# Row buffers and one-hot matrices of the edge stage of a graph layer: six buffers of one tile, one-hot matrices made by twos

## What is computed

```python
msgs = x[src]
out = x @ root + bias
for r in range(R):
    mask = (edge_type == r)
    sums = segment_sum(msgs * mask[:, None], dst, N)
    cnt = segment_sum(mask, dst, N)
    out = out + (sums / maximum(cnt, 1)[:, None]) @ weight[r]
z = concat([out, x], 1) @ w_gate + b_gate
h = tanh(out) * z + x * (1 - z)
```

## Time and profile before

| what | value |
|---|---|
| median of three runs | 1840.62 us (1838.92 to 1841.84) |
| the profiled execution, its own time | 1834.11 us |
| its span, first to last instruction | 1832.4 us |
| PE busy | 1708.7 us (93%) in 7873 matmuls |
| DVE busy | 1096.1 us (60%) in 1444 instructions |
| ACT busy | 727.0 us (40%) |
| POOL busy | 749.1 us (41%) |
| mean granted PE clock | 0.972 |
| moved by DMA | 339.69 MB, mean 185 GB/s |

### The profile page before, as it was taken

How to read it: one execution, slowest core, us unless ns; L and a number is a source line. 1 busy time by engine, 2 the same in 40 slices (tenths; PEclk the granted TensorE clock), 3 DMA queues, 4 the chain that set the end, 5 groups by cost and what they waited for, 6 DMA issues and landing times. The chain is left out here.

```text
span 1832.4 us, 22117 instructions
## 1 busy us (share of the span) xinstructions
PE 1708.7 (93%) x7873; PEld 1401.7 (76%) x7873; DVE 1096.1 (60%) x1444; ACT 727.0 (40%) x1230; POOL 749.1 (41%) x663
## 2 busy tenths in 40 slices
PE   7999999999999999999899999989789957999993
PEld 6888888888888888888687777767678846878882
DVE  8555556665464342424399998889799876334200
ACT  2316656631231313121256565556522103454551
POOL 1011222226775656302255545555265515455531
PEclk9999999999999999999899999999899968999997
DMA  5236555566224343434788888888745436877545
GB/s 204 92 121 224 169 176 178 161 193 199 87 92 156 115 152 114 148 127 143 245 281 297 266 283 277 265 290 273 263 170 171 149 115 218 227 186 208 138 88 150
DMA packets 141050, 339.69 MB, mean 185 GB/s; under 512 B 19332, under 2 KB 35764, under 8 KB 140864
## 3 DMA queue, kind: packets, MB, share of 16 engines
q0 software_dynamic: 50816, 159.29, 29.2%
q1 hardware_dynamic: 90128, 179.00, 29.1%
HBM read 241.19 MB, written 102.15 MB: 187 GB/s over the span
## 5 line engine op out<-in xcount | busy, mean ns | idle before, releaser
L1053 POOL DMA_INDIRECT gathered<-Y,edge_row x184 | 211.9, 1152 | 230.2 <-PE banks L1212 191.5
L623 ACT ACTIVATE ghi<-gathered,edge_w 128x1024 fp32r<-128x1024 f32 x184 | 211.7, 1152 | 171.7 <-DMA gathered<-Y,edge_row 162.0
L942 DVE SCALAR_TENSOR_TENSOR glo<-gathered,edge_w,ghi 128x1024 fp32r<-128x1024 f32 x184 | 232.2, 1282 | 48.3 <-ACT ghi L623 47.4
L1029 POOL DMA_INDIRECT edge_w<-INV,edge_key x184 | 207.9, 1130 | 116.8 <-DMA edge_w<-INV,edge_key 85.3
L1070 PE MATMUL banks<-whi,xhi 128*128 128x512 f32 x640 | 253.4, 396 | 0.4 <-DVE xlo L766 0.4
L1072 PE MATMUL banks<-whi,xlo 128*128 128x512 f32 x640 | 250.4, 391 | 0.0
L1071 PE MATMUL banks<-wlo,xhi 128*128 128x512 f32 x640 | 250.2, 391 | 0.0
L1211 PE MATMUL banks<-ghi,sel 128*128 128x512 f32 x368 | 149.0, 405 | 23.8 <-DVE glo L942 23.1
L573 ACT ACTIVATE ring_hi<-raw_chunk 128x512 fp32r<-128x512 f32 x112 | 66.5, 625 | 207.5 <-PE banks L1174 125.6
L1212 PE MATMUL banks<-glo,sel 128*128 128x512 f32 x368 | 144.5, 393 | 0.0
L1072 PEld LDWEIGHTS banks<-whi,xlo 128*128 128x128 f32 x640 | 120.6, 188 | 25.5
(11 more groups left out here) (316 smaller groups left out, 3677.6 us busy)
## 6 DMA issues: line engine op xcount, KB each, us to landing
raw<-in_L_ffn_w SPq DMA_DIRECT2D x24, 1024.0 KB, 10.2
Y<-y_out SPq DMA_DIRECT2D x80, 256.0 KB
t_set<-in_L_gnn_weight POOLq DMA_DIRECT2D x64, 256.0 KB
TW<-t_set POOLq DMA_DIRECT2D x64, 256.0 KB
raw_chunk<-TW SPq DMA_DIRECT2D x64, 256.0 KB
w_stage<-in_L_gnn_weight SPq DMA_DIRECT2D x30, 512.0 KB, 5.0
raw_chunk<-in_L_gnn_weight SPq DMA_DIRECT2D x48, 256.0 KB
Y<-half_v SPq DMA_DIRECT2D x40, 256.0 KB
```

Source lines behind the costliest of these rows:

```text
L623: nc.scalar.activation(ghi[:, t % HR], gath[t % GR][:], ACT.Copy, scale=edge_w[:, t:t + 1]).then_inc(g_hi, 1)
L942: v.scalar_tensor_tensor(glo[t % GR][:], gath[t % GR][:], edge_w[:, t:t + 1], ghi[:, t % HR].bitcast(F32), ALU.mult, ALU.subtract).then_in ...
L1029: nc.gpsimd.indirect_dma_start(out=edge_w[:, t:t + 1], out_offset=None, in_=INV, in_offset=bass.IndirectOffsetOnAxis(ap=edge_key[:, t:t + ...
L1053: nc.gpsimd.indirect_dma_start(out=gath[t % GR][:], out_offset=None, in_=Y, in_offset=bass.IndirectOffsetOnAxis(ap=edge_row[:, t:t + 1], a ...
```

## The change

The row buffers become six (GR = 6). The sixth lies where four of the one-hot matrices were, and has a landing semaphore of its own (pool_moved gets a sixth entry, with no earlier transfers). The ring of one-hot matrices becomes SR = 4 long, made SG = 2 tiles at a time, and moves behind the accumulator, into the room of half_v4 (so DVE waits for that buffer's last store, row_moved[4], in place of those of buffers 2 and 3). The place of places in DVE's order changes with SG. A semaphore of POOL's first lines is saved by counting its two steps on consts, which two engines wait for once.

```diff
-        pool_moved = [sem(f"pool_transfers_landed{i}") for i in range(5)]
-        t_moved, w_gathered = pool_moved[:TS], pool_moved[TS:]
-        pool_moves = [...] + [ET // 2] * 2
+        pool_moved = [sem(f"pool_transfers_landed{i}") for i in range(6)]
+        t_moved, w_gathered = pool_moved[:TS], pool_moved[TS:TS + 2]
+        pool_moves = [...] + [ET // 2] * 2 + [0]
...
-        GR, HR, SR, SG = 5, 3, 8, 4
-        gath_at = [OFF_W0 + 16 * KB + 4 * D * i for i in range(GR - 1)] + [z3.start]
+        GR, HR, SR, SG = 6, 3, 4, 2
+        gath_at = [OFF_W0 + 16 * KB + 4 * D * i for i in range(4)] + [z3.start, OFF_YOUT + 4 * KB]
...
-        sel = Zone(OFF_YOUT + 4 * KB, 4 * KB).put("sel", [P, SR, P], F32R)
+        sel = Zone(after_acc, 4 * P * SR).put("sel", [P, SR, P], F32R)
...
-                    dve.wait_ge(consts, 5)
+                    dve.wait_ge(consts, 7)
...
-                for i in range(2, 4):
-                    dve.wait_ge(row_moved[i], OUTS * (R - R0))
+                dve.wait_ge(row_moved[4], OUTS * (R - R0))
...
-                        if t % SG == 2 and SR <= t + 2 < ET:
-                            places((t + 2) // SG)
+                        if t % SG == SG - 1 and SR <= t + SR - SG + 1 < ET:
+                            places((t + SR - SG + 1) // SG)
...
-                built = sem("built")
-                nc.gpsimd.memset(ident[:], 0.0).then_inc(built, 1)
-                nc.gpsimd.memset(tri[:], 1.0).then_inc(built, 1)
-                pool.wait_ge(built, 2)
+                nc.gpsimd.memset(ident[:], 0.0).then_inc(consts, 1)
+                nc.gpsimd.memset(tri[:], 1.0).then_inc(consts, 1)
+                pool.wait_ge(consts, 2)
...
-                pe.wait_ge(consts, 5)
+                pe.wait_ge(consts, 7)
```

More of the change, by code:

```diff
@@ L264, in right @@
             return w[low * HALF + k * P:low * HALF + (k + 1) * P, wide * HALF:(wide + 1) * HALF]
-        pool_moved = [sem(f"pool_transfers_landed{i}") for i in range(5)]
-        t_moved, w_gathered = pool_moved[:TS], pool_moved[TS:]
-        pool_moves = [4 * len(range(i, 8 * (R - R0), TS)) for i in range(TS)] + [ET // 2] * 2
+        pool_moved = [sem(f"pool_transfers_landed{i}") for i in range(6)]
+        t_moved, w_gathered = pool_moved[:TS], pool_moved[TS:TS + 2]
+        pool_moves = [4 * len(range(i, 8 * (R - R0), TS)) for i in range(TS)] + [ET // 2] * 2 + [0]
         T_STEPS = 8 * (R - R0)
```

## The result

The kernel after takes 1929.0 us, the median of six runs (1926.51 to 1934.46), and the kernel before 1838.68 us in as many (1835.89 to 1841.84): a ratio of 1.0494, 95% interval 1.0476 to 1.0512. It is 90 us slower. The forecast was 1943.5 us, range 1915 to 1980.

What follows compares the result with a forecast made beforehand. PE and DVE were taken as nearly full at once in the edge stage. 88 periods of 5.41 us plus 13.6 for wlo and the ends lengthen it by 102.8 us; 103 added to the median gives 1943.5 us, range 1915 to 1980.

Steps and rivals of the forecast that it cites:

- The condition: In places: DVE asks for tile t, whose glo it has just finished, so it stands still at every odd t, 90 times.
- The price of one wait: Edge stage, from glo's end to DVE's next start with a free PE: 1.47 us, bounds 1.32 and 1.65.
- The rest of the period: DVE's order after the wait: sel to glo 0.33, glo to acc 1.20, acc to glo 1.13; period 5.41 us a pair.
- The path to the end: Edge stage: 88 periods of 5.41 from 913.5, plus wlo, put t = 179 at 1403.2 and the last matmul at about 1412.0.
- The 12 wlo: DVE in the edge stage: same serial order, 1.13 us each, covering nothing, 13.6 us in all.
- rival A: PE in the edge stage: idle gaps also lower its clock; +41 us (1985) if a fifth of pairs, all about 2150; chance 0.11.
- PE keeps up: Edge stage: PE reaches tile t + 2 at 4.12, glo's signal at 4.09, so PE adds next to nothing to the period.
- The sixth buffer: POOL's gathers, one tile earlier: DVE's 37.8 us of waiting for late rows end inside the new waits, no further gain.
- Rival B: Edge stage: the sixth buffer wins and the wait costs nothing, a gain of some 20 to 30 us, 1815; chance 0.02.
- The sum: Edge stage's last matmul moves from 1309.26 to about 1412.0, +102.8 us; 103 added to the median gives 1943.5 us.
- Rival C: Edge stage: the wait's price is off, 1910 with low bounds and half the wlo hidden, 1984 with high; chance 0.10 each side.
- sel by twos: DVE making one-hot matrices two tiles at a time: 92 x 0.33 less 46 x 0.60, 3 us more.

Runs made afterwards that it cites:

- the last three runs: Kernel before with one-hot matrices by twos behind glo of odd t, by fours there, and by twos behind acc of even t: ratios 0.9966, 0.9981, 1.0001.

## Why the prediction was right, step by step

**The condition.** The reading of the index was the decisive step: DVE asks for the tile that it has handed over that moment, 90 times. The trace has exactly 90 such waits, and the run with one index changed takes them all away. It was right.

**The price of one wait** was taken as 1.47 us and is 1.34. The row for it was the acc at the stage's end, which started 0.15 us after the PE. sel starts 0.03 us after. This is no accident of one row: in the eleven traces whose tiles have four matmuls the last acc starts 0.14 or 0.15 us after the PE. acc computes its address from a register first, and that instruction (64 ns, just ahead of each acc) is my explanation of the difference. acc also has a second wait, for the acc before it (acc_done). No run tested either. The term was 0.13 us too large, and 88 periods make 11 us of it. This is the largest part of the 14.5 us by which the forecast was too high.

**The rest of the period** was right to 0.02 us: sel to glo 0.35 (0.33), glo to acc 1.19 (1.20), acc to glo 1.13. The period is 5.29 us against 5.41. sel of 256 elements takes 0.426 us, the 0.420 of rows 6.

**The path to the end.** t = 179 has its sel at 1396.2, forecast 1403.2. From 913.26 to there it is 88 periods of 5.295, thus 466.0, and 16.9 more. The 12 wlo were put at 13.6. The other 3 us are rival A in small: 86 of the 90 waits took 1.33 to 1.36 us, two are the first two, and two took 2.90, 1.55 more each, both right where the clock was low. Windows of the PE in the kernel after:

```profile
980.00:990.00 10.00, 8.63 (x36) 1.00 0.75 231
990.00:1000.00 10.00, 7.74 (x27) 0.83 0.65 206
1000.00:1010.00 10.00, 7.53 (x31) 1.00 0.84 243
1010.00:1020.00 10.00, 6.82 (x23) 0.83 0.85 283
1020.00:1030.00 10.00, 8.65 (x36) 1.00 0.65 181
```

The granted clock fell twice here, each time right behind 2.25 us in which the PE was idle (until 995.6 and 1016.5), where a wlo stood between sel and the glo that the PE waited for. The matmuls behind it start 0.43 us apart, the 1.2 GHz level:

```profile
1016.47 0.70 PE L1209 MATMUL banks<-ghi,sel 128*128 128x512 f32 x1 [2.25 <-DVE glo L942]
1016.97 0.63 PE L1210 MATMUL banks<-glo,sel 128*128 128x512 f32 x1
1017.40 0.63 PE L1209 MATMUL banks<-ghi,sel 128*128 128x512 f32 x1
```

It was back at 1.00 in the next window, and stayed there from 1020 to 1400. So the gaps of 0.4 to 1.1 us in every period didn't pull the clock down, as rows 8 had it, and neither did five of 1.55 to 1.61 us. Nor does a gap of 2.25 us always: with five buffers and the wait kept, the same gap at the same place in the order left the clock at 1.00, and the matmuls behind it start 0.23 us apart:

```profile
1010.00:1020.00 10.00, 6.82 (x29) 1.00 0.78 262
1015.69 0.47 PE L1209 MATMUL banks<-ghi,sel 128*128 128x512 f32 x1 [2.26 <-DVE glo L942]
```

What decides between the two isn't shown. The Trainium skill's rule ("TensorE: Matmul & The Clock Gate", section "A second HAM failure mode: psum-queue depth-cycling"), by which brief idle times between groups of matmuls make the clock swing when they come often enough, is not borne out by the regular gaps here. Rival A as priced, +41 us, didn't happen. Its argument from rows 8 was a little loose: 4.4 of 5.4 us is 0.81, where the windows read had 0.83 to 0.90.

**PE keeps up.** In the kernel after this held: 86 of the 90 waits have the free PE's value. It doesn't hold of itself, as the run with the wait in the kernel before showed, where the same reasoning came out 15 to 25 us short. One reading beside it was off by one tile, at no cost: ghi(t + 2) waits for tile t - 1, not t, so ACT had more time than the prediction gave it.

**The sixth buffer** was costed as no gain, and is none here: with five it takes 1930.67. Rival B's mechanism was sound as well, and its point of decision well placed. With a lag restored the time is 1816.4, where B had 1815. (The buffer lies where all eight one-hot matrices were, 4 KB per partition, not four of them as the part on the change says. No time hangs on that.)

**The sum.** The stage was forecast to end at 1412.0 and ended at 1405.3. That is 6.7 of the 14.5 us. Of the rest, 1.9 is the median of the kernel before, 1840.6 in the three runs that the forecast had and 1838.7 in six. The last 6 are the step from the stage to the total: the forecast put the stage's growth, read from one trace, whole on the median, but the stages of the two traces end 96.1 us apart and the medians lie 90.3 apart. Each profiled execution lies some 5 us from its kernel's median, to opposite sides. Where in an execution those lie, no run shows. Rival C covers such a miss in size, and the result lies within the range, 1 us below the forecast's own narrow range (1930 to 1960).

**sel by twos** was costed at +3 us. As the last three runs show, it costs nothing measurable, and made in the new place it saves the kernel before 0.3%. In the kernel after, no run separates it from the wait.

## What to carry to other kernels

When a ring is refilled as far as it goes, the refill asks for the consumer's newest tile. On the engine that also feeds that consumer this closes a loop of waits between both. Ask one item later: a lag of one tile was enough here, and it turned 5% slower into 1.2% faster, with the same instructions. Read the count in each wait against what its own engine has just handed over, before costing any of the rest. And value a buffer only once such a wait is gone: the sixth one was worth 0 us beside the wait and 17 us without it.

## What the runs showed of the hardware that was not expected

- From the shown end of the PE's last matmul to the start of the DVE instruction that waits for it, it is 0.03 us to sel and 0.15 us to acc.
- A wait for the other engine has no fixed price: the same question cost 1.34 us each at every pair and 1.88 us each (82.6 us in 44) at every second pair, where the PE still had one or two products ahead of the tile.
- The PE's clock held at 1.00 through gaps of 0.4 to 1.1 us in every period and five of 1.55 to 1.61, and fell to 0.83 in two windows of 10 us, each with a gap of 2.25 us. In the kernel with five buffers and the wait, one of two such gaps left it at 1.00.
